# A decoder layer on one core: a partition holds two neighbouring rows, so that tiles move in 4096-byte packets

## The reference, cut to what matters

```
x = x + attn(layernorm(x))                        # 16 heads, out @ Wff.T + bff
x = x + xattn(ctx, ctx, layernorm(x))             # one head of 512, biases bv, bq, bo
x = x + ffn(layernorm(x))                         # 2048 keys, top 8, 8 rows of aux_values gathered

ffn: scores = rq @ rk.T / sqrt(48) + mask;  top_scores, top_idx = top_k(scores, 8)
     agg    = sum_k softmax(top_scores)[k] * aux_values[top_idx[k]]
     gate   = sigmoid(w1 * clip(log1p(var) / mean(log1p(var)) * 0.5 + 2.5 * sigmoid(learned)) + b)
     out    = hidden + gate * agg
```

## Time and profile before

| | |
|---|---|
| three runs, median (lowest to highest) | 2807.72 us (2807.22 to 2808.9) |
| the profiled execution's own time | 2788.23 us |
| its span | 2786.2 us |
| busy: TensorE, VectorE, ACT, GpSimd | 2556.4, 2146.0, 1431.3, 683.1 us |
| DMA packets, bytes | 131542, 358.87 MB |
| of these in queue 0 (GpSimd's) | 63520, 160.60 MB, 24.4% of 16 engines |
| in queue 1 (SP's) | 63188, 192.15 MB, 23.6% |
| in queue 10 (ACT's) | 4784, 5.46 MB, 0.6% |

### The profile page before, as it was taken

The page is one execution under the profiler, slowest core; times in us unless marked ns, Lnnn a source line. Parts: engine busy times, 40 slices in busy tenths (PEclk is TensorE's granted clock), DMA queues, the critical chain, the costliest instruction groups (busy, mean ns, idle before and its releaser), DMA issues.

```text
span 2786.2 us, 56938 instructions
## 1 busy us (share of the span) xinstructions
PE 2556.4 (92%) x19090; PEld 2104.0 (76%) x19090; DVE 2146.0 (77%) x4207; ACT 1431.3 (51%) x4247; POOL 683.1 (25%) x650
## 2 busy tenths in 40 slices
PE   6899999999999999999999999999999999999730
PEld 4578878887888788878887888778888887788520
DVE  5456888888888888888888888888888888887552
ACT  2345554555555545555555455555554555555252
POOL 0001222222222222222222222222222222222254
PEclk9899999999999999999999999999999999999955
DMA  5223354454544444444444445444445454444799
GB/s 189 53 80 80 107 132 121 128 137 130 133 121 112 130 125 123 138 131 131 128 111 128 131 113 138 131 131 131 115 126 134 106 139 130 132 130 111 202 205 178
DMA packets 131542, 358.87 MB, mean 129 GB/s; under 512 B 21906, under 2 KB 26514, under 8 KB 123267
## 3 DMA queue, kind: packets, MB, share of 16 engines
q0 software_dynamic: 63520, 160.60, 24.4%
q1 hardware_dynamic: 63188, 192.15, 23.6%
q10 hardware_dynamic: 4784, 5.46, 0.6%
HBM read 316.37 MB, written 41.78 MB: 129 GB/s over the span
## 4 chain that ended last, share of the span: by engine, by line
PE 74%; DVE 8%; ACT 7%; issue 7%; DMA 2%; POOL 1%; DVEq 0%; ACTq 0%; POOLq 0%; SPq 0%
PE psX L1144 43%; PE psA L1144 13%; PE psA L1153 5%; PE psF L1144 4%; PE psA L1210 4%; DVE top L999 3%; PE psA L1233 2%; ACT paT L640 2%; PE psX L1153 2%; ACT sc L640 1%; DMA vg<-in_L_ffn_aux_values,idx 1%; ACT xT_hi L663 1%; DVE xmax L948 1%; PE psF L1153 1%; DVE idx L1002 1%
## 5 line engine op out<-in xcount | busy, mean ns | idle before, releaser
L589 POOL DMA_INDIRECT vg<-in_L_ffn_aux_values,idx x512 | 491.7, 960 | 1550.5 <-DVE agg L1028 1053.8
L684 ACT ACTIVATE pa<-psA,nmax 112x224 f32<-112x224 f32 x1024 | 444.6, 450 | 197.8 <-DVE nmax L917 194.5
L917 DVE TENSOR_REDUCE nmax<-psA 112x4 f32<-112x896 f32 x256 | 267.1, 1085 | 100.9 <-PE psA L1210 100.9
L1144 PE MATMUL psX<-big,gT 128*112 128x375 f32 x1024 | 333.4, 478 | 0.6 <-ACT gT L711 0.6
L1028 DVE SCALAR_TENSOR_TENSOR agg<-vg,wt,agg 112x512 f32<-112x512 f32 x406 | 303.8, 748 | 9.2
L1144 PE MATMUL psX<-pT,cx 125*128 125x224 f32 x1536 | 299.1, 355 | 0.0
L1144 PEld LDWEIGHTS psX<-pT,cx 125*128 125x128 f32 x1536 | 288.0, 190 | 4.0 <-issue 0.3
L932 DVE TENSOR_TENSOR pa<-pa,rsum 112x896 f32<-112x896 f32 x256 | 279.4, 1091 | 8.8
L1144 PEld LDWEIGHTS psX<-big,gT 128*112 128x112 f32 x1024 | 175.2, 176 | 126.0 <-issue 0.9
L1153 PE MATMUL psA<-ident,pa 112*112 112x112 f32 x2048 | 227.2, 262 | 19.5 <-DVE oT_lo L895 19.4
L640 ACT COPY paT<-psA 112x448 f32<-112x448 f32 x512 | 237.2, 560 | 11.4 <-PE psA L1153 9.4
(11 more groups left out here) (220 smaller groups left out, 5957.0 us busy)
## 6 DMA issues: line engine op xcount, KB each, us to landing
big<-in_ctx_t SPq DMA_DIRECT2D x32, 1500.0 KB, 8.1
cx<-in_ctx SPq DMA_DIRECT2D x32, 1344.0 KB
xa<-in_x SPq DMA_DIRECT2D x64, 224.0 KB
centered<-in_x_t SPq DMA_DIRECT2D x32, 448.0 KB, 4.6
x<-in_L_attn_bff POOLq DMA_DIRECT2D x32, 448.0 KB, 5.7
x<-cb_scratch POOLq DMA_DIRECT2D x32, 448.0 KB, 5.9
x<-in_x SPq DMA_DIRECT2D x31, 448.0 KB
out<-x SPq DMA_DIRECT2D x30, 448.0 KB, 3.1
```

The lines of the kernel that those rows point to most:

```text
L589: pool.indirect_dma_start(vg[:, c % SLOTS, k, :], None, aux_values, bass.IndirectOffsetOnAxis(ap=idx[:, t, n:n + 1], axis=0))\
L684: last = nc.scalar.activation(pa[:, t, h, :], psA[0:R, h, t * S:(t + 1) * S], ACT.Exp, bias=nmax[:, k % 2, h, t:t + 1], accum_out=rsum[:, ...
L917: nc.vector.tensor_reduce(nmax[:, k % 2, h:h + 2, :], psA[0:R, h:h + 2, 0:T * S].rearrange("p h (t s) -> p h t s", t=T), AX_X, ALU.max, ne ...
L1144: last = nc.tensor.matmul(dst, stationary, moving, start=n == 0, stop=n == len(pairs) - 1)
```

## The change

Tile t, partition r is now row 2r + t of the batch everywhere, by `pairs`; `tiles` is gone. A partition's two rows are neighbours in DRAM and in the SBUF tile, 4096 bytes in one piece. Tokens of the transposed input are in the order t, r, and the moments are stored in that order, float by float. `cb` and `attn_bff` stand twice in a row in DRAM scratch, so that a bias add reads 4096 bytes at once too; `bff` gets there by a DMA that ACT issues, and GpSimd waits for it once. The store of `agg` tiles goes to every second row.

```diff
-        moments_dram = nc.dram_tensor("moments_scratch", [B, R, T], F32).ap()
-        cb_dram = nc.dram_tensor("cb_scratch", [1, D], F32).ap()
+        moments_dram = nc.dram_tensor("moments_scratch", [B, T, R], F32).ap()
+        cb_dram = nc.dram_tensor("cb_scratch", [T, D], F32).ap()
+        bff_dram = nc.dram_tensor("bff_scratch", [T, D], F32).ap()
...
         def over_rows(v):
-            return v.partition_broadcast(R).unsqueeze(1).to_broadcast([R, T, D])
-
-        def tiles(a):
-            return a.rearrange("(t r) d -> r t d", r=R)
+            return v.rearrange("t d -> (t d)").partition_broadcast(R).rearrange("r (t d) -> r t d", t=T)
 
         def pairs(a):
             return a.rearrange("(r t) d -> r t d", t=T)
...
-                sp.dma_start(cb_dram, cb[0:1, :]).then_inc(cb_stored, 16)
+                sp.dma_start(cb_dram, cb[0:T, :]).then_inc(cb_stored, 16)
...
-                sp.dma_start(row(moments_dram, b), rstd["N"][:, :]).then_inc(moments_stored, 16)
+                with nc.allow_non_contiguous_dma(reason="moments, one by one"):
+                    sp.dma_start(row(moments_dram, b).rearrange("t r -> r t"), rstd["N"][:, :]).then_inc(moments_stored, 16)
...
-                sp.dma_start(spread[:, :], row(moments_dram, b).rearrange("r t -> (r t)").partition_broadcast(P))\
+                sp.dma_start(spread[:, :], row(moments_dram, b).rearrange("t r -> (t r)").partition_broadcast(P))\
...
-                sp.dma_start(x1[:, :, :], tiles(row(x, b))).then_inc(xr_loaded, 16)
+                sp.dma_start(x1[:, :, :], pairs(row(x, b))).then_inc(xr_loaded, 16)
...
-                    sp.dma_start(tiles(row(agg_dram, b))[:, t, :], agg[:, :]).then_inc(agg_stored, 16)
+                    sp.dma_start(pairs(row(agg_dram, b))[:, t, :], agg[:, :]).then_inc(agg_stored, 16)
...
             def bias_x(b, _):
+                if isinstance(b, int) and b == 0:
+                    pool.wait_ge(bff_stored, 16)
                 pool.wait_ge(xr_loaded, 16 * (b + 1))
                 apart(pool)
-                pool.dma_start(x1[:, :, :], over_rows(attn_bff), accum_op=ALU.add).then_inc(xr_biased, 16)
+                pool.dma_start(x1[:, :, :], over_rows(bff_dram), accum_op=ALU.add).then_inc(xr_biased, 16)
...
-                pool.dma_start(tiles(row(out, n)), late_tile[n], accum_op=ALU.add).then_inc(late_stored[k], 16)
+                pool.dma_start(pairs(row(out, n)), late_tile[n], accum_op=ALU.add).then_inc(late_stored[k], 16)
...
-            act.dma_start(x1[:, :, :], tiles(row(x, 0))).then_inc(xr_loaded, 16)
+            act.dma_start(bff_dram, attn_bff.partition_broadcast(T)).then_inc(bff_stored, 16)
+            act.dma_start(x1[:, :, :], pairs(row(x, 0))).then_inc(xr_loaded, 16)
...
-    a = np.asarray(inputs["x"]).reshape(B, S, C, P).transpose(0, 3, 2, 1)
+    a = np.asarray(inputs["x"]).reshape(B, R, T, C, P).transpose(0, 4, 3, 2, 1)
```

More of the change, by code:

```diff
@@ L257, in build @@
         x_loaded, xt_loaded, xr_loaded, ctx_loaded, cxT_loaded = (sem(f"{n}_loaded") for n in ("x", "xt", "xr", "ctx", "cxT"))
-        moments_stored, moments_spread, cb_stored = sem("moments_stored"), sem("moments_spread"), sem("cb_stored")
+        moments_stored, moments_spread = sem("moments_stored"), sem("moments_spread")
+        cb_stored, bff_stored = sem("cb_stored"), sem("bff_stored")
         xt_scaled, xT_split, xr_biased = sem("xt_scaled"), sem("xT_split"), sem("xr_biased")
@@ L499, in store_whole @@
                     sp.wait_ge(merged, n - WHOLE + 1)
-                    sp.dma_start(tiles(row(out, n)), late_tile[n]).then_inc(late_stored[LATE + n - DIRECT], 16)
+                    sp.dma_start(pairs(row(out, n)), late_tile[n]).then_inc(late_stored[LATE + n - DIRECT], 16)
             def store_base(b, _):
@@ L505, in store_base @@
                 sp.wait_ge(base_ready, b + 1)
-                sp.dma_start(tiles(row(out, b)), x2[:, :, :]).then_inc(base_stored, 16)
+                sp.dma_start(pairs(row(out, b)), x2[:, :, :]).then_inc(base_stored, 16)
             def store_agg(b, c):
@@ L534, in load_agg @@
                 sp.wait_ge(agg_stored, 16 * T * (n + 1))
-                sp.dma_start(late[k], tiles(row(agg_dram, n))).then_inc(late_loaded[k], 16)
+                sp.dma_start(late[k], pairs(row(agg_dram, n))).then_inc(late_loaded[k], 16)
             pipeline(sp, {("Z", "load"): load_agg, ("Z", "scale"): store_whole, ("W", "split"): after_split, ("W", "keys"): after_keys,
@@ L571, in bias_x1 @@
                 apart(pool)
-                pool.dma_start(x1[:, :, :], over_rows(cb_dram.rearrange("a d -> (a d)")), accum_op=ALU.add).then_inc(x1_biased, 16)
+                pool.dma_start(x1[:, :, :], over_rows(cb_dram), accum_op=ALU.add).then_inc(x1_biased, 16)
             def add_base(b, _):
```

## The result

| | before | after |
|---|---|---|
| median (lowest to highest) | 2807.47 us (2806.89 to 2808.9), 4 runs | 3021.44 us (3018.99 to 3022.7), 4 runs |
| the profiled execution, its span | 2788.23, 2786.2 us | 3018.99, 3017.2 us |
| busy: TensorE, VectorE | 2556.4, 2146.0 us | 2653.2, 2150.6 us |
| packets in queue 0, in queue 1 | 63520, 63188 | 52992, 56470 |

The ratio is 1.076, with an interval of 1.0742 to 1.0779: the kernel became 7.6% slower. The forecast, 2803.0 us with a range of 2796 to 2811, was wrong in sign and in size. The packets did grow as planned (queue 0 lost 10528 of them, 112 for each of 94 DMAs).

The account below looks back on a forecast made before the run. The prediction took TensorE to bound the loop and the DMA engines the tail from 2670 us on. Tail adds -3.8, tail loads -1.5 and start +0.6 sum to -4.7 us, giving 2803.0 us from 2807.72, range 2796 to 2811.

Parts of the forecast that it names:

- What bounds the kernel: Whole kernel: TensorE bounds the loop, DMA engines the tail from 2670 us; in the loop no touched transfer is waited for.
- Start, moments store (L470): First two batches: 7 more packets an engine cost +0.6 us, bounds +0.1 and +1.4; in the loop, nothing.
- sign of being wrong: Loop moving over 2 us; also an adding packet over 377 or under 310 ns, or a tail no longer full.
- The same at the start itself: Start: batch 0's moments store takes 7.8 to 8 us in place of 7.31; batch 1's grows by 7 x 8.4 ns.
- ACT's extra DMA: Start, doubled `bff`: one more issue of 0.45 us on ACT, hidden with 0.66 us left; +0.45 us if uncovered.
- Tail, 30 adds: Adds on the output after 2670 us: each saves 7 x 18 ns, together -3.8 us, bounds -1.8 and -11.3.
- Tail, 29 loads: Loads of `agg` in the tail: larger packets save -1.5 us, bounds 0 and -1.7.
- GpSimd: Descriptor writing: the 64 bias DMAs may each give back 0.25 us; counted as 0 in loop and tail.
- D: Rival on packet size: packets do not grow, only a limit on adding would split them; 2806.8 us, chance 0.08.
- C: Rival, tail adds: 4096-byte adds overlap less, 418 ns a packet, deciding from 377 ns; 2821.9 us, chance 0.10.
- A: Rival, tail: bytes alone count, so the tail saves nothing and the start costs 0.6 us; 2808.3 us, chance 0.17.
- B: Rival, end of tail: slowest engines give back more, half their lag, a further -5.1 us; 2797.9 us, chance 0.23.

Follow-up runs that it names:

- the version with 8-byte pairs: Changed kernel with the moments stored as before, 8 bytes a partition, VectorE reading at a two-float step: ratio 0.9997 to before, on another chip 0.9977.
- the floats alone: Kernel before with only the moments put in the order t, r and stored float by float, tiles still in 2048-byte packets: 3005.74 us against 2782.16, ratio 1.0807.
- the halved adds: Changed kernel with 8-byte moments, each of the tail's 30 adds split into two DMAs of 2048 bytes a partition: 2784.71 us, ratio 1.001 to before.
- second profile of before: Kernel before, unchanged, profiled again on the chip of the runs beside it; the kernel's median there is 2782.16 us.
- the two profiles of one chip: Kernel before against one whose moments are late with no float stored singly: spans 2779.8 and 2997.4 us.

## Why the prediction was wrong, step by step

- *What bounds the kernel: "in the loop no transfer that the change touches is waited for."* True of before, and of no use as it was put. That a transfer is not waited for tells that its room is above zero, not how large it is. The room was some 0.5 to 1.1 us, and could have been read beforehand from SP's and VectorE's timelines.
- *Start, moments store (L470), "7 x 8.4 ns for batch 1", and "in the loop the same store has time".* **This is the step that failed.** The term counted packets and took the landing to be their end. The packets cost what it said, 8.5 ns each; the store takes 7.2 us in place of 2.7. At 5.2 us more of lateness against some 1 us of room, the loop's term, put at nothing, came to 6.7 us a batch. Bounds of +0.1 and +1.4 us were drawn from packets alone and could not hold it. The forecast's own sign of being wrong, a loop that moves by more than 2 us, is the one that came true. The earlier trace rows already showed the gap: 8 packets an engine at 8.4 ns are 0.07 us, and the store took 2.6.
- *The same at the start itself.* Batch 0's store took 10.5 us in place of 7.31, forecast 7.8 to 8, batch 1's 7.27 in place of 3.92. `centered` came at 28.76 us (25.56 before), and `xT_hi` at 30.29 (26.69).
- *ACT's extra DMA, "an issue, 0.45 us as its neighbour".* Too low: the copy of `bff` (L638) takes 1.17 us in the changed kernel and 1.16 in the version with 8-byte pairs. There it is hidden with next to nothing left: ACT's table load ends at 26.12 us, `centered` at 26.15. In the changed kernel the table load ended at 30.28 us, 0.4 us after `centered`, and that is in the chain. ACT's loads ran longer there, above all `b1c`'s issue: 7.30 us, and 7.81 with the floats alone, against 4.04 before and 3.56 with pairs. The floats are what those two have in common; more is not shown.
- *Tail, 30 adds: -3.8 us.* The size agrees with the halved adds (3.6 to 4.75 us) and with 109.3 to 109.6 us from the gate to the end against 112.2 to 116.4, with the reservations given there. The sum had 18 ns for each two packets made one; the medians give 28, which would be 5.9 us in all.
- *Tail, 29 loads: -1.5 us.* Not seen. It should have brought the gate forward, and the gate stands at 2666.30 us in the second profile of before and at 2666.03 in that of the version with pairs; a part of 1.5 us could hide between two single profiles.
- *GpSimd.* A bias add's descriptors (L574, L572 before) take 929 ns in place of 1214, near the 0.25 us that was taken, and free the engine for nothing in the loop, as said.
- *The rivals.* D fell: every add is 112 packets. C fell: 328 ns, not 377. A, no gain in the tail, has the tails against it, but not the whole kernel's time: 0.9997 (0.9988 to 1.0006) on one chip can't be told from no change, 0.9977 (0.9968 to 0.9986) on the other can. B in full, without the start's term, is 5.3 + 5.1 = 10.4 us, and both intervals exclude it (at most 3.3 and 9.0 us); its last stretch, a few engines finishing alone, did not halve either: 9.5 us at a DMA share of 0.50 with pairs, 9.8 at 0.42 in the second profile of before. C, the only slower rival, put its mechanism in the adds; none had the moments' path, which is the one place where the change makes pieces smaller. And no term anywhere gave TensorE's clock a price, which turned some 128 us of waiting into 218 us (the two profiles of one chip).

## What to carry to other kernels

A small DMA that someone waits for is priced by the median from issue to landing of its own shape, not by its packets: where a change alters how pieces lie in DRAM, measure that store alone. Before a path is called hidden, subtract: when its result is there, when its user comes to it, and what that user holds up. Where TensorE is the bound, a pause of some microseconds in each batch costs the pause and then some of the clock, here two fifths of the loss.

## What the runs showed that was not expected

- A store's landing goes by the pieces that fall into 256 bytes of DRAM: 1.3 to 1.5 us up to 16, 2.0 with 21, 2.6 to 3.2 with 32, 5.7 to 6.5 with 64, for 4, 8 or 12 bytes a piece, and the same for 64 and for 112 floats in a row.
- A store of 224 single floats held up a load issued right behind it by some 3 us, more than pairs of 8 bytes did.
- VectorE multiplies 128x896 floats in 1.08 us with an operand read at a step of 8 bytes, and in 1.80 us at a step of 16.
- TensorE came out of a 5.06 us pause at 1.2 GHz and was back at 2.4 by 1493 us; the trace has 28 stretches at the lower level between 130 and 2580 us. The Trainium skill, TensorE: Matmul & The Clock Gate, has the clock at just these two levels ("What's actually happening") and names waits for DMAs between groups of matmuls as what lowers it ("HAM oscillation — how this bites in real kernels"); the 0.63 and 0.39 us of one matmul agree.

Open remain the mechanism behind the store's law, and why the same packets gain 0.03% on one chip and 0.23% on another. Of the 22 us by which the profile on the second chip is longer (2797.1 against 2775.5 us of span, the same kernel), all lies ahead of the gate: from there to the end it is 109.3 and 109.5 us.
